# Adding the decay and query terms of the chunk transitions on TensorE instead of VectorE

## The reference, cut to what matters

```python
def step(S, inp):
    qt, kt, vt, gt, bt = inp
    S = S * jnp.exp(gt)[..., None, None]
    v_new = vt - jnp.einsum('bhk,bhkv->bhv', kt, S)
    S = S + bt[..., None, None] * (kt[..., :, None] * v_new[..., None, :])
    o = jnp.einsum('bhk,bhkv->bhv', qt, S)
    return (S, o)
...
x = _layernorm(x + attention(x))
x = _layernorm(x + ternary(x) @ w_rram.T)
```

## Time and profile before

| what | value |
|---|---|
| median of 3 runs | 350.73 us (350.22 to 351.06) |
| profiled execution, its own time | 353.02 us |
| its span in the profile | 351.2 us |
| matmul rows of TensorE, and as many weight loads | 6956 |
| busy, TensorE | 252.8 us |
| busy, VectorE | 268.5 us |
| busy, ScalarE | 146.8 us |
| mean granted TensorE clock | 0.86 |

### The profile page before, as it was taken

One profiled execution on the slowest core, in us unless ns is written; L12 is line 12 of the kernel. 1 busy time (PEld: TensorE's weight loads), 2 busy tenths in 40 slices (PEclk: granted clock), 3 DMA queues, 4 the chain that ended last, 5 costly groups with the idle time before them and its releaser, 6 DMA issues.

```text
span 351.2 us, 15117 instructions
## 1 busy us (share of the span) xinstructions
PE 252.8 (72%) x6956; PEld 178.0 (51%) x6956; DVE 268.5 (76%) x660; ACT 146.8 (42%) x271; POOL 9.2 (3%) x14
## 2 busy tenths in 40 slices
PE   2978943986479958958699589776928458967571
PEld 1435421666455535756455356665607357755441
DVE  0688999563999995969999887589999960546966
ACT  1497763255463602734636214635423024024031
POOL 2110000001000000010000000100000000000000
PEclk9999976698989985999989955999876757969898
DMA  7900000000000002000001020000010002000101
GB/s 231 359 0 2 3 1 0 4 4 6 4 5 4 0 0 63 6 4 6 6 4 60 0 63 4 4 7 4 4 60 0 2 5 63 6 5 4 60 1 60
DMA packets 8031, 9.82 MB, mean 28 GB/s; under 512 B 1568, under 2 KB 7072, under 8 KB 7968
## 3 DMA queue, kind: packets, MB, share of 16 engines
q1 hardware_dynamic: 6480, 8.39, 7.2%
q10 hardware_dynamic: 1488, 0.47, 0.5%
HBM read 6.76 MB, written 2.10 MB: 25 GB/s over the span
## 4 chain that ended last, share of the span: by engine, by line
PE 53%; DVE 22%; issue 18%; ACT 5%; DMA 1%; DVEq 0%; SPq 0%; ACTq 0%
PE fr L322 15%; PE pj L335 10%; PE pj L350 5%; PE pg L322 5%; PE pc L322 4%; DVE conv_buf L958 4%; PE po L322 3%; PE pc L479 3%; PE po L479 2%; PE pj L509 2%; DMA xt<-x_t 1%; PE pj L367 1%; DVE tok_buf L970 1%; DVE ss L991 1%; DVE stats L1222 1%
## 5 line engine op out<-in xcount | busy, mean ns | idle before, releaser
L335 PE MATMUL pj<-xt,wproj 128*128 128x512 f32 x96 | 53.6, 706 | 8.4 <-DMA xt<-x_t 6.4
L958 DVE SCALAR_TENSOR_TENSOR conv_buf<-raw,wconv,conv_buf 128x512 f32<-128x512 f32 x72 | 53.3, 755 | 4.9 <-ACT conv_buf L663 3.2
L335 PEld LDWEIGHTS pj<-xt,wproj 128*128 128x128 f32 x96 | 20.0, 220 | 31.0 <-issue 24.0
L662 ACT ACTIVATE raw<-pj 128x512 f32<-128x512 f32 x24 | 14.3, 596 | 34.7 <-PE pj L335 34.7
L1088 DVE TENSOR_TENSOR mq<-fr,ad 128x512 f32<-128x512 f32 x12 | 8.3, 692 | 26.5 <-PE fr L322 26.5
L350 PE MATMUL pj<-xt,wproj 128*128 128x512 f32 x48 | 25.1, 664 | 4.6 <-ACT conv_buf L663 4.6
L322 PE MATMUL fr<-x_t,x 32*32 32x16 f32 x768 | 11.5, 209 | 21.6 <-issue 21.6
L322 PEld LDWEIGHTS fr<-x_t,x 32*32 32x32 f32 x768 | 10.9, 151 | 24.3 <-issue 24.3
L322 PE MATMUL fr<-kga,wu 32*32 32x64 f32 x768 | 14.7, 228 | 7.2 <-issue 7.2
L350 PEld LDWEIGHTS pj<-xt,wproj 128*128 128x128 f32 x48 | 10.0, 213 | 16.4 <-issue 8.4
L727 ACT ACTIVATE s_sb<-po 128x192 f32<-128x192 f32 x12 | 4.0, 330 | 32.8 <-PE po L322 32.8
(11 more groups left out here) (181 smaller groups left out, 578.2 us busy)
## 6 DMA issues: line engine op xcount, KB each, us to landing
xt<-x_t SPq DMA_DIRECT2D x1, 1536.0 KB, 11.4
res<-x SPq DMA_DIRECT2D x3, 512.0 KB, 4.1
out<-hid_buf SPq DMA_DIRECT2D x6, 256.0 KB, 2.1
wproj<-w_proj SPq DMA_DIRECT2D x1, 1024.0 KB, 7.4
xt<-x_t SPq DMA_DIRECT2D x1, 512.0 KB, 5.0
kq<-x SPq DMA_DIRECT2D x1, 512.0 KB, 3.8
wout<-w_out SPq DMA_DIRECT2D x1, 384.0 KB, 11.7
cst<-consts ACTq DMA_DIRECT2D x1, 305.5 KB, 11.4
```

The source lines that it names most:

```text
L335: mm = pe.matmul(pj[:, j % 2, :], wproj[:, t, j * P:(j + 1) * P], xt[:, t, k * TOK:(k + 1) * TOK], start=(t == 0), stop=(t == KT - 1))
L662: act.activation(raw[:, j, :, TAPS - 1:], bank, ACT.Copy)
L958: e = dve.scalar_tensor_tensor(out=conv[:, d, :, :], in0=raw[:, d, :, m:m + T], scalar=wconv[:, j, m:m + 1], in1=conv[:, d, :, :], op0=ALU ...
```

## The change

`transitions(k, b)` first multiplies the 128x128 identity with the 512 columns of `ad` that belong to bank b and writes the result to the bank; the 32 small products then accumulate onto it. `transition_sum` on VectorE is gone. In its place ScalarE copies each bank to `mq` in `transition_out(k, b)`. The order of VectorE and ScalarE changes with it: VectorE does five tap tiles, then `kq_to_tokens`, the sixth tap tile and `factors`; ScalarE puts the copies between silu 0, 1 and 2, `square` goes to c = 2, silu 3 to c = 1, silu 4 and 5 to c = 3 and 4. TensorE waits for decay_in and qe_done in `transitions`, VectorE for mq_mm in `scaled_operands`, ahead of writing `ad` anew.

```diff
--- before.py
+++ after.py
@@ -420,10 +420,15 @@
                 if b == 0:
                     after(pe, kg_done, 1, k, 1)
                     after(pe, at_done, 1, k, 1)
+                    after(pe, decay_in, 1, k, 1)
+                    after(pe, qe_done, 1, k, 1)
+                pe.matmul(fr[:, b, :], cst[:, C_IDENT:C_IDENT + P],
+                          ad[:, :, :, :].rearrange("p c g x -> p (c g x)")[:, b * MB * 64:(b + 1) * MB * 64],
+                          start=True, stop=False, skip_group_check=True)
                 for n in range(b * MB, (b + 1) * MB):
                     i = n - b * MB
                     mm = by_head(fr[:, b, i * 64:(i + 1) * 64], wu[:, n, 0:DK], kga[:, k % 2, n // G3, n % G3, :],
-                                 start=True, stop=True)
+                                 start=False, stop=True, skip_group_check=True)
                 mm.then_inc(mq_mm, 1)
 
             def new_state(k, c):
@@ -722,6 +727,11 @@
                 act.activation(wu[:, b * WB:b * WB + n, :].rearrange("p u x -> p (u x)"), wu_bank[b][:, 0:n * 96],
                                ACT.Copy).then_inc(wu_out, 1)
 
+            def transition_out(k, b):
+                after(act, mq_mm, b + 1, k, 3)
+                act.activation(mq[:, b * MB:(b + 1) * MB, :].rearrange("p u x -> p (u x)"), fr[:, b, :],
+                               ACT.Copy).then_inc(mq_in, 1)
+
             def state_out(k, c):
                 after(act, s_mm, c + 1, k, NC - 1)
                 act.activation(s_sb[:, (c + 1) % 2, :], s_bank[c % 2][:, 0:G3 * DV], ACT.Copy).then_inc(s_done, 1)
@@ -806,8 +816,14 @@
                     weight_part(2)
                 state_out(k, 0)
                 if front:
-                    for j in range(3):
-                        silu(k + 1, j)
+                    silu(k + 1, 0)
+                transition_out(k, 0)
+                if front:
+                    silu(k + 1, 1)
+                transition_out(k, 1)
+                transition_out(k, 2)
+                if front:
+                    silu(k + 1, 2)
                 for c in range(1, NC):
                     if c < NC - 1:
                         state_out(k, c)
@@ -818,9 +834,11 @@
                             heads_square(k, c // 2)
                         continue
                     if c == 1:
+                        silu(k + 1, 3)
+                    if c == 2:
                         square(k + 1)
-                    if 3 <= c < 6:
-                        silu(k + 1, c)
+                    if 3 <= c < 5:
+                        silu(k + 1, c + 1)
                     if c >= 5:
                         heads_square(k, c - 5)
                     if c == NC - 1:
@@ -1008,6 +1026,8 @@
 
                 def rows(v):
                     return v.rearrange("p (g c) -> p g c", g=G3).unsqueeze(3).to_broadcast([P, G3, NC, DK])
+                if not first(k):
+                    after(dve, mq_mm, 3, k - 1, 3)
                 dve.tensor_tensor(by_group(kr[:, :, :, 0:DK]), kq_tok[:, :, 0, :, :], rows(fk[:, :]),
                                   ALU.mult).then_inc(kc_done, 1)
                 dve.tensor_tensor(qe_tok.rearrange("p (g c) d -> p g c d", g=G3), kq_tok[:, :, 1, :, :],
@@ -1080,15 +1100,6 @@
                                              op0=ALU.mult, op1=ALU.subtract))
                 dve.tensor_tensor(right, right, scale(norm[:, :]), ALU.mult).then_inc(tt_done, 1)
 
-            def transition_sum(k, b):
-                after(dve, mq_mm, b + 1, k, 3)
-                after(dve, qe_done, 1, k, 1)
-                after(dve, decay_in, 1, k, 1)
-                units = slice(b * MB, (b + 1) * MB)
-                dve.tensor_tensor(mq[:, units, :].rearrange("p u x -> p (u x)"), fr[:, b, :],
-                                  ad[:, :, :, :].rearrange("p c g x -> p (c g) x")[:, units, :].rearrange(
-                                      "p u x -> p (u x)"), ALU.add).then_inc(mq_in, 1)
-
             def head_eps(k):
                 dve.tensor_scalar(eps_o[:, :, :], ss[:, :, 1, :], EPS_O, EPS_O * EPS_K, ALU.mult, ALU.add)
 
@@ -1267,22 +1278,14 @@
                 if not first(k):
                     ternary(k - 1)
                 if front:
-                    for j in range(first(k), 3):
+                    for j in range(first(k), 5):
                         conv_taps(k + 1, j)
-                for b in range(3):
-                    transition_sum(k, b)
-                    if not front and b < 2:
-                        feed_forward_sum(k - 1, b)
-                if front:
                     kq_to_tokens(k + 1)
-                    for j in range(3, CONV_TILES):
-                        conv_taps(k + 1, j)
+                    conv_taps(k + 1, 5)
                     factors(k + 1)
                 if not first(k):
-                    if front:
-                        feed_forward_sum(k - 1, 0)
-                    if front:
-                        feed_forward_sum(k - 1, 1)
+                    feed_forward_sum(k - 1, 0)
+                    feed_forward_sum(k - 1, 1)
                     after(dve, ffn_in, 2, k - 1, 2)
                     moments(hid)
                 if not front:
```

## The result

The changed kernel takes 343.73 us in the median of 4 runs (342.39 to 347.09), the kernel before 350.48 of 4 runs beside it: ratio 0.985, 95% interval 0.980 to 0.989. The forecast was 346.3, a gain of 4.4 us; measured are 5.4 by the ratio (3.8 to 6.9), while the two medians are 6.75 apart. It is faster, inside the range.

The account below looks back on a forecast made before the run. VectorE was taken to bound the front of turns 0 to 2 from kq_to_tokens on. Turn terms 1.9 + 1.7 + 2.6 - 1.8 = 4.4 us off the median 350.73 gave 346.3, range 342.5 to 351.3.

Parts of the forecast that it names:

- VectorE bound turns 0 to 2 from kq_to_tokens on: Turns 0 to 2, front of the next pair: ending kq_to_tokens and six tap tiles sooner shortens the turn, up to slack.
- a turn's gain is 4.5 minus the lateness of kq_to_tokens: VectorE, turns 0 to 2: two tap tiles go ahead, 4.5 us, minus lateness of 1.6, 2.8 and 1.9.
- The new wait for silu 2: VectorE ahead of kq_to_tokens: silu 2 stands behind the third copy, a wait of about 3 us in turns 1 and 2.
- The gaps take in part of the products: TensorE's transitions: a block of 128 small pairs takes some 3.5 us anyway, so products partly run in its gaps.
- The product's price: TensorE: one identity product costs 0.88 us at full clock, 1.86 at half clock.
- Turn 0's cap: Turn 0, head sum: squares end some 0.2 us later, so the gain of 2.9 us is capped at 1.9.
- the forecast loss: Turn 3, TensorE's chain of states: first block 1.4 us late, second 0.4, a loss of 1.8.
- The clock as a rival: TensorE ahead of the merge: less idle time avoids half clock behind it, 2 to 4 us more gain, 343; chance 0.12.
- the terms: Gains of 1.9, 1.7 and 2.6 us in turns 0, 1 and 2, and a loss of 1.8 in turn 3.
- the slower one (products in full): TensorE's transitions: gaps are fixed pauses, products add fully, about 2.7 us slower, 353.4; chance 0.16.
- half clock in turn 0's transitions: Turn 0: clock falls anyway, transitions end 3.1 us late, turn loses 1.0 instead of gaining 1.9; 349.2, chance 0.09.
- The one in which waits only change places: Turns 1 and 2: silu 2 another 2 us late, kq_to_tokens 4 to 4.8 late, VectorE wins nothing; 350.6, chance 0.09.

Follow-up runs that it names:

- before_again: The kernel before, profiled again with no edit; 349.43 us against 350.22, ratio 0.996.
- the pair of 2.7 and 17.9 us: Kernel before plus three dropped large products a turn (354.30 us, ratio 1.008), and kernel before with the transitions' small products done twice (369.19 us, ratio 1.051).
- after_again: The changed kernel, timed and profiled again with no edit; 345.04 us, ratio 0.987 to the kernel before.
- products_only: Kernel before plus three 128x512 products a turn on TensorE, results dropped, nothing else changed; 354.30 us, ratio 1.008.
- fill_only: Kernel before with the fourth tap tile ahead of the first sum and the fifth behind it, nothing moved to TensorE or ScalarE; 342.59 us, ratio 0.979.
- fill_again: Kernel before with two tap tiles ahead of the later sums, timed once more; 342.91 us, ratio 0.979.
- silu2_first: Changed kernel with silu 2 ahead of the three copies on ScalarE; 343.03 us, ratio 0.980 to the kernel before.
- the move in the old order: Changed kernel with silu 0 to 2 ahead of the copies, square at c = 1, three tap tiles ahead of kq_to_tokens and three behind; 342.35 us, ratio 0.980.
- the move with the filling: Changed kernel with silu 0 to 2 ahead of the copies, square at c = 1, four tap tiles ahead of kq_to_tokens, two behind; 342.24 us, ratio 0.978.

## Why the prediction came out right, and where its steps did not

*VectorE bound turns 0 to 2 from kq_to_tokens on: shown.* From the head sum to x16 takes 70.3 to 70.4 us in three turns in every profile, and a turn's gain is 4.5 minus the lateness of kq_to_tokens. Against before_again, which has it 16.0, 15.0 and 15.0 us into turns 0 to 2, the two profiles of the changed kernel have it 1.1, 3.2 and 2.2 later in the mean, so 3.4, 1.3 and 2.3; measured are 3.3, 1.3 and 2.3. I had put the lateness at 1.6, 2.8 and 1.9. The new wait for silu 2, forecast at about 3 us in turns 1 and 2, is 4.25 and 2.38 in one profile, 3.53 and 3.43 in the other.

*The gaps take in part of the products: shown* by the pair of 2.7 and 17.9 us and by the packets. The product's price was a little low: the pitch of a third is 2.08 us with 1.04 for its 64 small rows, so 1.04 and not 0.88. In turn 1 that, and the phase of the blocks, made the transitions end later by 1.6 us (mean of two, against before_again) and not by 1.1.

*Turn 0's cap failed.* I let the squares end 0.2 us later than the 33.8 us into the turn that they took before. They ended at 32.4 and 32.8. I had the clock full through the transitions of turn 0, and there it was. The stretches of the earlier trace rows in the changed kernel:

```profile
76.00:82.00 6.00, 4.89 (x162) 3.01 (x164) 4.17 (x6) 4.27 (x8) 0.00 (x0) 1.00 0.02 5
82.00:86.00 4.00, 4.00 (x220) 3.15 (x212) 0.00 (x0) 1.58 (x4) 0.00 (x0) 1.00 0.02 4
```

TensorE is busy 4.89 of 6 us where it was 2.81, and the clock is at 1.00 in both stretches. It fell later in the turn instead: 0.72 over 91 to 97 us, and 0.67 in after_again. fill_only, without products, had 1.00 in these two stretches as well, so this isn't proof that the products hold it. Nor is it shown that the clock brought the squares forward: products_only has 1.00 there too and ends them at 33.9, fill_only at 32.0. Why they came early stays open. Gain 3.3 instead of 1.9.

*Turn 3: the forecast loss didn't show, and isn't refuted either.* The transitions there ended 0.6 us later into the turn (mean of two, against before_again) instead of 1.8, and from the third copy to the last head sum the changed kernel took 16.05 us in both profiles, before_again 17.8 from the third sum. The same stretch behind it, before_again, products_only and the changed kernel in this order:

```profile
306.30:318.30 12.00, 9.05 (x402) 8.19 (x392) 6.89 (x21) 3.53 (x9) 0.00 (x0) 0.72 0.03 5
```

```profile
311.80:323.80 12.00, 7.59 (x362) 5.97 (x352) 7.44 (x22) 4.43 (x12) 0.00 (x0) 1.00 0.02 4
```

```profile
302.00:314.00 12.00, 7.78 (x353) 6.06 (x343) 7.84 (x22) 4.82 (x12) 0.00 (x0) 1.00 0.02 4
```

Part of this chain ran at half clock (mean 0.72) in both profiles of the kernel before and at full clock in all with products. Without products the mean is 0.97 in fill_only and 1.00 in fill_again, so full clock there doesn't need them.

Three more kernels have the same turn 3 as the changed one, instruction for instruction: silu2_first, the move in the old order, and the move with the filling. Their third copies stand 1.8, 1.2 and 1.6 us later into the turn than before_again's third sum, near the 1.8 I had forecast, and their turn 3 takes 64.1, 63.5 and 64.2 us to the end, against 62.3 and 63.8 in the kernel before and 61.4 and 62.0 in the changed one. So the gain of 0.6 is within what executions differ by, and the size of turn 3's term stays open.

The clock as a rival I had placed behind the merge. There it is refuted: the project tile ahead of the second merge takes 3.78 and 3.76 us in turns 0 and 1 of both profiles of the changed kernel, at half clock as before (3.78). It changed in turns 0 and 3.

*A cost I had not seen: the merges.* x16 to the next turn took 33.6 us in both profiles, against 32.7 and 31.9. One place is seen in turn 1, at the merge of the changed kernel:

```profile
199.54 2.75 PE L322 MATMUL fr<-x_t,x 32*32 32x16 f32 x191 [4.51 <-issue]
203.65 0.18 PE L322 MATMUL fr<-x_t,x 32*32 32x16 f32 x1 [1.36 <-issue]
```

The last of 192 rows fell behind a gap, so the whole merge ended 1.4 us late. Added instructions shift where every later gap falls. But silu2_first and the move with the filling have that late last row too (behind gaps of 1.93 and 2.36), and their three stretches from x16 to the next turn take 31.5 and 31.9 us, no more than before_again's. So the 1.6 us aren't a fixed cost of the added instructions; where they come from stays open.

So the sum was 4.4 and the terms were 1.9, 1.7, 2.6 and -1.8; measured they are 3.3, 1.3, 2.3 and +0.6, with -1.6 at the merges and -0.4 at the start, 5.4 between the spans. That the sum came within 1.0 of this is partly luck: turn 0 and turn 3 came out better than their terms by 1.4 and 2.4 us, and turns 1 and 2, the merges and the start worse. Of the rivals, the slower one (products in full) is refuted by products_only, and half clock in turn 0's transitions by the stretches above. The one in which waits only change places has a grain of truth: the new wait of VectorE is longer than the one removed (4.25 against 2.77 us in turn 1), and what pays is the work that went ahead of it.

The Trainium skill, Runtime: NRT & Kernel Launch, section Instruction fetch mechanics, says that blocks of 256 instructions are fetched while the current one executes, at a cost that is mostly hidden. The trace agrees with the block and the overlap: the packet of 151.45 to 152.41 comes while TensorE executes. It disagrees with "mostly hidden": two blocks of 128 small pairs start 4.00 us apart though the first executes in 1.99.

## What to carry to other kernels

Before moving work off an engine that waits, look whether work that it does later, and that is ready, fits into the wait: here a few lines of reordering gave 2.1%, the move with its new instructions 1.3 to 1.5%. Where TensorE runs hundreds of tiny products, count instructions, not nanoseconds: a large product among them costs only a part of its time until the gap is full (2.7 us for 13 here), and its second copy most of it (7 to 8 us for some 12). When a wait is taken out, name the next one and its margin, and let that margin move with the change too.

## What was not expected of the hardware

A block of 256 TensorE instructions (128 matmul rows and as many loads) took 3.3 to 4.1 us from gap to gap in the kernel before, with gaps of mostly 1.1 to 2.0 that end 1.2 to 1.6 us after a packet of the instruction queue, whereas three products of 128x512 a turn, 13 us in all, cost 2.7 us in the end. And the granted clock in the chain of turn 3 was 0.72 in the mean in both profiles of the kernel before and 1.00 in those with three more large products a turn, but also 0.97 and 1.00 in the two of the filled kernel, which has none; what decides it at so similar a load stays open.
